# Masking on VectorE instead of TensorE: row maxima of batches 2 and 3 in layer 0 of a two-layer transformer kernel

## The reference

```python
qkv = jnp.einsum('bsd,od->bso', x, w_project)
...
att = jnp.einsum('bhqd,bhkd->bhqk', q, k) / math.sqrt(HEAD_DIM)
causal = jnp.triu(jnp.ones((s, s), dtype=bool), k=1)
att = jnp.where(causal[None, None, :, :], jnp.float32(-1000000000.0), att)
att = jax.nn.softmax(att, axis=-1)
out = jnp.einsum('bhqk,bhkd->bhqd', att, v)
```

## Time and profile before

| | |
|---|---|
| median of 3 runs | 256.35 us (256.03 to 258.0) |
| profiled execution, its own time | 255.42 us |
| its span (first to last instruction) | 253.5 us |
| TensorE matmuls busy | 240.6 us, 95% |
| TensorE weight loads busy | 216.3 us, 85% |
| VectorE busy | 204.3 us, 81% |
| ScalarE busy | 161.4 us, 64% |
| GpSimd busy | 167.1 us, 66% |
| mean granted clock of TensorE | 0.997 |

### The profile page before, as it was taken

One profiled execution on the slowest core, in us unless ns is written; L12 is line 12 of the kernel. 1 busy time (PEld: TensorE's weight loads), 2 busy tenths in 40 slices (PEclk: granted clock), 3 DMA queues, 4 the chain that ended last, 5 costly groups with the idle time before them and its releaser, 6 DMA issues.

```text
span 253.5 us, 6724 instructions
## 1 busy us (share of the span) xinstructions
PE 240.6 (95%) x2398; PEld 216.3 (85%) x2398; DVE 204.3 (81%) x599; ACT 161.4 (64%) x290; POOL 167.1 (66%) x218
## 2 busy tenths in 40 slices
PE   8998989999999999999999898998999999999991
PEld 8997967877789989989999897765788888999990
...
GB/s 164 277 193 203 216 175 241 152 120 79 76 98 109 109 129 119 85 145 144 187 85 189 3 122 189 31 153 145 0 45 3 4 3 0 3 35 8 3 0 124
DMA packets 23312, 26.39 MB, mean 104 GB/s; under 512 B 3184, under 2 KB 18288, under 8 KB 23280
## 3 DMA queue, kind: packets, MB, share of 16 engines
...
...
## 4 chain that ended last, share of the span: by engine, by line
PE 71%; POOL 6%; DVE 5%; DMA 5%; ACT 5%; issue 4%; SPq 2%; POOLq 0%; ACTq 0%
PE psum L566 9%; PE psum L567 8%; PE psum L568 8%; PE psum L686 6%; PE psum L661 5%; PE psum L741 5%; PE psum L742 5%; DMA k_stack<-k_part 3%; PE psum L629 3%; PE psum L689 2%; PE psum L633 2%; PE psum L664 2%; POOL hidden L1253 2%; PE psum L775 2%; PE psum L638 2%
## 5 line engine op out<-in xcount | busy, mean ns | idle before, releaser
L857 ACT ACTIVATE probs<-psum 128x768 f32<-128x768 f32 x64 | 49.1, 809 | 11.9 <-PE psum L667 5.9
L1253 POOL TENSOR_TENSOR hidden<-hf,hidden 128x512 fp32r<-128x512 f32 x24 | 31.6, 1320 | 13.5 <-ACT hidden L899 13.5
L1221 POOL TENSOR_SCALAR_AFFINE_SELECT probs<-probs 128x512 f32<-128x512 f32 x48 | 32.3, 688 | 10.1 <-ACT probs L857 9.7
L1009 DVE TENSOR_REDUCE block_max<-psum 128x6 f32<-128x768 f32 x32 | 28.9, 946 | 6.0 <-PE psum L633 5.9
L661 PE MATMUL psum<-q_stack,k_stack 98*128 98x256 bf16 x128 | 28.6, 274 | 2.1 <-DMA q_stack<-maxT_lo 1.0
L1020 DVE CUSTOM_DVE_ANT_0 masked<-psum,mask 128x256 bf16<-128x256 f32 x64 | 26.7, 418 | 1.6 <-issue 0.9
L1106 DVE SCALAR_TENSOR_TENSOR hf<-th,psum 128x512 f32<-128x512 f32 x28 | 18.9, 677 | 9.8 <-ACT th L888 3.9
L566 PE MATMUL psum<-xT_hi,gu_hi 128*128 128x256 f32 x88 | 25.3, 288 | 0.0
L567 PE MATMUL psum<-xT_lo,gu_hi 128*128 128x256 f32 x88 | 24.9, 283 | 0.0
L568 PE MATMUL psum<-xT_hi,gu_lo 128*128 128x256 f32 x88 | 24.9, 283 | 0.0
L664 PE MATMUL psum<-q_stack,k_stack 98*128 98x128 bf16 x128 | 24.7, 218 | 0.0
...
## 6 DMA issues: line engine op xcount, KB each, us to landing
q_stack<-q_part SPq DMA_DIRECT2D x48, 128.0 KB, 2.7
k_stack<-k_part SPq DMA_DIRECT2D x48, 128.0 KB, 2.4
...
```

Source lines behind the costliest of these rows:

```text
L857: nc.scalar.activation(probs[(n - 1) % 4][:, :, :], place(key)[:, :, 0:T + P], ACT.Exp, scale=SC).then_inc(exp_done, 1)
L1009: nc.vector.tensor_reduce(block_max[b % 2][:, 2 * i:2 * i + 2, 1:4], both(key)[:, :, 0:3 * P].rearrange("p j (c t) -> p j c t", t=P), mybi ...
L1221: pool.affine_select(out=diag, in_=diag, compare_op=ALU.is_ge, fill=0.0, base=0, pattern=[[0, 2], [0, 2], [1, P]], channel_multiplier=-1). ...
L1253: pool.tensor_tensor(hidden[(n - 1) % NHID][1][:, :, :], hf[n % 2][:, :].rearrange("p (a t) -> p a t", a=2), hidden[(n - 1) % NHID][0][:, ...
```

## The change

`MASKED_BY_PE` goes from 4 to 2. Batches 0 and 1 of layer 0 keep the mask by TensorE; batches 2 and 3 of layer 0 get the form that layer 1 has. On TensorE the third matmul of a head goes for 32 heads. On VectorE 16 reductions of two heads become 64 masked maxima, and MB:020 and MB:030 go. All five lists of steps and the table of banks are written anew, for layer 1 also. The steps in the lists are otherwise the same.

```diff
-MASKED_BY_PE = 4
+MASKED_BY_PE = 2
 TENSOR_STEPS = """
...
-    V:020 S:011-3 ST:000-1 S:014-5 ST:002-3 S:016 PV:000-1 ST:004-7 S:017 S:020-2 MX:010 PV:002-3 S:023-4 V:030
-    ST:010 S:025-6 ST:011 S:027 ST:012-4 MX:020 S:030 PV:010-1 S:031-2 ST:015 O:000 ST:016-7 ST:020 PV:012 S:033-4
-    ST:021 PV:013 ST:022 S:035-6 XT:000 ST:023 S:037 PV:020 ST:024-6 PV:021 MX:030 ST:027 GU:000 ST:030 PV:022-3
+    V:020 S:011-4 ST:000 S:015 ST:001-3 S:016 ST:004 PV:000-1 S:017 ST:005-6 S:020 ST:007 S:021 MX:010 S:022-3
+    PV:002-3 S:024-5 V:030 ST:010-2 S:026-7 ST:013 PV:010-1 ST:014 S:030 MX:020 S:031 ST:015-6 PV:012 S:032 ST:017
+    O:000 ST:020-1 PV:013 ST:022-4 S:033-6 PV:020 XT:000 S:037 PV:021 ST:025-7 MX:030 GU:000 PV:022-3 ST:030-1 O:010
...
 VECTOR_STEPS = """
-    XPARTS:000 PREPA:000-1 XPARTS:010 QK:000-1 XPARTS:020 XPARTS:030 QK:010 PREPA:002 QK:011 QK:020-1 PREPA:003
-    S:000-7 MB:000 S:010 MX:000 QK:030-1 S:011-6 SCALES:000 UT:000 IV:000 S:017 MB:010 S:020-1 MX:010 S:022 YM:000
-    S:023-4 UT:001 S:025-7 IV:001 MB:020 YM:001 YB:000 MX:020 S:030 UT:010 PREP0:004-5 S:031-2 O:000 PREP0:006
-    S:033-4 UT:011 S:035-7 MB:030 XT:000 MX:030 IV:010-1 YM:010-1 YB:010 GU:000 UT:020 IV:020 UT:021 YM:020 IV:021
+    XPARTS:000 PREPA:000-1 XPARTS:010 QK:000 PREPA:002-3 XPARTS:020 QK:001 QK:010-1 QK:020-1 XPARTS:030 S:000-7
+    MB:000 QK:030 S:010 MX:000 QK:031 S:011-5 SCALES:000 S:016 UT:000 S:017 MB:010 IV:000 S:020-1 MX:010 S:022-5
+    UT:001 IV:001 YM:000-1 S:026 YB:000 S:027 S:030 MX:020 UT:010 PREP0:004-5 S:031-2 O:000 PREP0:006 UT:011 S:033-6
+    IV:010 S:037 XT:000 YM:010 MX:030 IV:011 YM:011 YB:010 UT:020 GU:000 UT:021 IV:020-1 YM:020-1 YB:020 O:010
...
 SYNC_STEPS = """
-    LOAD:001 LOAD:003 QK:000 LOAD:002 QK:001 MID:000-1 LO:000-1 QK:010 MID:010 LO:010 MID:011 QK:011 LO:011 LO:020
-    RAW:000-1 LOAD:000 MX:000 ML:000 LO:021 QK:020 MID:020-1 QK:021 RAW:002-3 MID:030 QK:030 MX:010 ML:010 MID:031
-    LO:030-1 QK:031 RAW:004-5 ML:020 MX:020 RAW:006-9 MX:030 ML:030 RAW:0010-25 QK:100 RAW:0026-27 MID:100 QK:101
+    LOAD:001 LOAD:003 QK:000-1 LOAD:002 LO:000 MID:000-1 LO:001 LO:010 QK:010-1 MID:010-1 LO:011 RAW:000-1 LOAD:000
+    LO:020-1 MX:000 ML:000 QK:020 MID:020-1 QK:021 RAW:002-3 QK:030 MX:010 ML:010 QK:031 MID:030-1 LO:030-1
+    RAW:004-5 MX:020 ML:020 RAW:006-10 ML:030 MX:030 RAW:0011-25 LO:100 RAW:0026 MID:100 RAW:0027 QK:100-1 MID:101
...
```

More of the change, by code:

```diff
@@ new lines @@
+    MX:110 QK:131 ST:104 PV:100-1 ST:105 S:121 ST:106-7 S:122-4 V:130 S:125-6 PV:102-3 ST:110-1 S:127 ST:112-5
+    PV:110 MX:120 ST:116 PV:111 S:130-1 PV:112 S:132 ST:117 O:100 ST:120-1 S:133 PV:113 ST:122 S:134 ST:123 S:135
+    PV:120 ST:124 S:136 XT:200 ST:125-6 PV:121 S:137 GU:100 MX:130 ST:127 GU:101 PV:122-3 ST:130-1 O:110 ST:132-3
+    GU:102-3 ST:134 PV:130-1 D:100-1 ST:135-7 XT:210 D:102 O:120 GU:110 PV:132-3 GU:111-2 D:103 XT:220 GU:113 GU:120
+    D:110 O:130 GU:121 D:111-2 GU:122-3 XT:230 D:113 D:120 GU:130-1 D:121-2 GU:132-3 D:123 D:130-3
@@ L109 @@
 """
 SCALAR_STEPS = """
-    XPARTS:000 PREPA:000-1 QK:000 XPARTS:010 PREPA:002 QK:001 SPLIT:000 XPARTS:020 XPARTS:030 SPLIT:001 QK:010-1
-    SPLIT:010 QK:020 SPLIT:011 QK:021 PREPA:003 V:000 SPLIT:020-1 V:010 QK:030-1 MX:000 PREP0:000 V:020 SPLIT:030-1
-    PREP0:001 ST:000-7 MX:010 PREP0:002-3 V:030 ST:010-3 MX:020 YT:000 ST:014-5 PREP0:004-5 ST:016-7 ST:020
-    PREP0:006 ST:021 LN:000 ST:022 PREP1:000 ST:023 XT:000 ST:024-5 MX:030 ST:026-7 PREP1:001-2 GU:000 ST:030-2
-    YT:010 AB:100 HI:000 AB:101 ST:033 GU:001 YT:020 AB:102-3 GU:002 ST:034 LN:010 ST:035 HI:001-2 AB:104-5 ST:036-7
@@ L121 @@
-    ST:125-6 CV:105-7 MX:130 ST:127 GU:100 YT:110 GU:101 ST:130-1 HI:100-1 ST:132-3 GU:102 LN:210 GU:103 YT:120
-    XT:210 ST:134-7 HI:102-3 GU:110-1 LN:220 HI:110 GU:112 YT:130 GU:113 HI:111-2 XT:220 GU:120 HI:113 LN:300 LN:230
-    GU:121 HI:120-1 XT:230 GU:122-3 GU:130 HI:122 GU:131 HI:123 HI:130-1 GU:132-3 HI:132-3 LN:310 LN:320
+    XPARTS:000 PREPA:000-1 QK:000 XPARTS:010 PREPA:002 QK:001 SPLIT:000 PREPA:003 XPARTS:020 QK:010 SPLIT:001
+    SPLIT:010 QK:011 QK:020 SPLIT:011 XPARTS:030 QK:021 V:000 V:010 SPLIT:020 QK:030 SPLIT:021 MX:000 QK:031
@@ L124 @@
+    GU:120-1 HI:113 HI:120 LN:300 LN:230 XT:230 GU:122 HI:121 GU:123 HI:122 GU:130 HI:123 HI:130 GU:131-2 HI:131
+    GU:133 HI:132-3 LN:310 LN:320
 """
 VECTOR_STEPS = """
[L126 to L128 removed]
@@ new lines @@
+    YT:020 HI:001-2 ST:034-7 LN:020 LN:100 YT:030 HI:010 TERN:100 LN:030 TERN:101 HI:011-2 TERN:102 SPLIT:100
+    TERN:103 LN:110 TERN:104 HI:020 TERN:105 SPLIT:101 HI:021 TERN:106 SPLIT:110 HI:022 SPLIT:111 HI:030-1 LN:120
+    HI:032 PREP1:003 LN:130 SPLIT:120-1 TERN:107 XC:100 ST:100 XC:110 ST:101-6 TERN:108 ST:107 SPLIT:130-1 ST:110-5
+    YT:100 ST:116-7 ST:120-1 LN:200 ST:122-3 TERN:109 ST:124-6 XC:120 ST:127 YT:110 TERN:1010-11 HI:100 ST:130-3
+    HI:101 LN:210 HI:102 YT:120 ST:134-6 XC:130 ST:137 HI:103 LN:220 HI:110 YT:130 HI:111-2 LN:300 LN:230 HI:113
@@ L149 @@
+    HI:120-3 LN:310 HI:130-3 LN:320 LT:130-1
 """
 SYNC_STEPS = """
-    LOAD:001 LOAD:003 QK:000 LOAD:002 QK:001 MID:000-1 LO:000-1 QK:010 MID:010 LO:010 MID:011 QK:011 LO:011 LO:020
-    RAW:000-1 LOAD:000 MX:000 ML:000 LO:021 QK:020 MID:020-1 QK:021 RAW:002-3 MID:030 QK:030 MX:010 ML:010 MID:031
-    LO:030-1 QK:031 RAW:004-5 ML:020 MX:020 RAW:006-9 MX:030 ML:030 RAW:0010-25 QK:100 RAW:0026-27 MID:100 QK:101
-    MID:101 LO:100-1 RAW:0028-29 QK:110 RAW:0030 LO:110 QK:111 MID:110-1 LO:111 MX:100 ML:100 QK:120-1 MID:120-1
@@ L157 @@
+    LO:101 RAW:0028 QK:110 RAW:0029-30 LO:110 MID:110-1 QK:111 LO:111 MX:100 ML:100 QK:120-1 MID:120-1 LO:120-1
+    RAW:0031-32 ML:110 MX:110 QK:130 MID:130-1 QK:131 LO:130-1 MX:120 ML:120 RAW:0033-34 MX:130 ML:130 LN:300 LN:310
+    LN:320 LT:130-1
 """
 BANKS = """
[7 rows of a table removed]
[7 rows of a table added]
 """
```

57 lines of the change are left out of this document (24 added, 33 removed), and 14 rows, old and new, of the table BANKS.

## The result

The changed kernel took 258.1 us (median of 20 runs, 256.48 to 260.26), the kernel before 255.62 beside it (20 runs, 253.86 to 260.15). The ratio is 1.0103, interval 1.0078 to 1.0128: about 1% slower, where 256.1 us, no change, was forecast. (The ratio leaves out runs over 1.5% above the fastest of their kernel, such as the one of 260.15, and so isn't the quotient of the medians.) The time lies in the range. The profiled execution of the changed kernel has a span of 255.6 us and a time of 257.53; before, 253.5 and 255.42.

The account below looks back on a forecast made before the run. TensorE sets the pace if VectorE keeps up from 43 to 68 us. -3.5 (TensorE's work) + 3.3 (its wait at MX:030) + 0 (the rest) = -0.2, so 256.1 us from 256.35; range 252.9 to 258.7.

Parts of the forecast that it names:

- TensorE's work, -3.5: Batches 2 and 3 of layer 0: 32 mask matmuls fewer at 0.11 us per head, 3.5 us less on TensorE.
- VectorE's work, +3.5: Layer 0: 16 steps at 0.24 us more, 3.8, less 0.3 for two dropped joins; net +3.5 us.
- Batch 2, "it ends where it ended": Batch 2's 1.9 us more on VectorE, covered by an earlier start from 3.2 us of idle time; costed at nothing.
- S:030 on VectorE at 53.0 to 53.6: Start of batch 3's maxima in layer 0, against 53.23 us before; taken as 53.2.
- the +0.3: ST:007 on TensorE, behind S:017 and S:020 in the new order, comes 0.3 us later.
- rival 3: Slot hand-over: TensorE waits at S:020, ST:007 and batch 3's transfers slide; 258.3 or 260.2 us, chance 0.16 for over 258.9.
- The wait at MX:030, +3.3: TensorE reaches MX:030 near 64.8 us and waits over 3 us for VectorE's S:037; stretch ends at 68.1 for 67.94.
- Layer 1, 0 with +-3.85: All re-ordered parts: between 3.85 us of VectorE waits won and as much lost; taken as 0.
- Rival 2: By weight loads TensorE has room and its work sets nothing; 256.4 us, no change, chance 0.13.
- Rival 1: TensorE's saving arrives whole: 252.9 us, or 254.6 for half; chance 0.22 for under 253.8.
- Rival 4: The dealt orders of layer 1 alone move the time by over 2.5 us; chance 0.02 each way.

Follow-up runs that it names:

- orders_alone: The changed kernel with the mask of all of layer 0 by TensorE again, its new orders and banks kept; ratio 1.0100 to the kernel before.
- batch3_old_orders: The kernel before, orders and banks kept, with the mask of batch 3 of layer 0 alone taken by VectorE; ratio 1.0000.
- three filled kernels: The changed kernel with extra TensorE matmuls in waits: 18 or 9 ahead of S:030, or 9 there and 9 ahead of ST:000; ratios 1.0040-1.0044 to before.
- new_then_old: The changed kernel up to GU:000 on every engine, the orders and banks of the kernel before from there; ratio 1.0212.
- filled_both_before: The kernel before with 9 extra TensorE matmuls ahead of ST:000 and 9 ahead of S:030; ratio 1.0144.
- old_transfers: The changed kernel with SyncE's transfers for batch 3's stacks in the order of the kernel before; ratio 1.0033 to the kernel before.

## Why the prediction was wrong

Its sum was -3.5 + 3.3 + 0. The main step that failed is that the new orders cover batch 2's 1.9 us on VectorE for nothing: they were charged 0.3 us for a later ST:007 and 0 to 0.4 for later maxima, with S:030 on VectorE at 53.2. They do cover those 1.9 us, but orders_alone shows that they cost 1.0% by themselves. In the changed kernel's profile the first part of that is at S:030's start, where the landing of the last transfer was put at 2.4 us and took 4.0. L649 of MX:030 came at 70.52 for the 68.1 of the sum. Of these 2.4 us, 1.2 are S:030's start on VectorE, 0.5 the stretch from there to S:037's end, where the clock had no price, and 0.7 what lies between S:037's end and L649.

- **TensorE's work, -3.5.** The 32 matmuls went (L633 has 32 executions, L1020 and L1023 96 each). Busy time from 43 to 68 us is 21.96, near the 21.5 named. No run shows a gain from it: batch3_old_orders takes 1.6 us from TensorE and gains nothing.
- **VectorE's work, +3.5.** Right. The busy column shows only +1.8, but the maxima of layer 0 alone are busy for 32.7 us where they were for 28.9; other passes took less. The stretch from S:030 to the end of S:037 was put at 14.8 us and took 15.33 (54.37 to 69.70) with the clock low, and 14.7 in the three filled kernels.
- **Batch 2, "it ends where it ended".** In the changed kernel it did: VectorE was through with it at 51.95 and then idle for 2.40 us; the kernel before came to S:030 at 53.23. S:020 came 2.45 us earlier. What failed is "I cost it at nothing" for the cover. With the old orders VectorE is full at 10.20 of 10.23 us, and the form costs 1.0% in batch 2, part of it the clock; with the new orders that cost is hidden, and the orders cost 1.0%. They replace one loss by the other. I had feared batch 3, which costs nothing by itself, and read rows 2 over 25 us, where VectorE had 1.6 us to spare; over the 10 us ahead of S:030 it had 0.03.
- **S:030 on VectorE at 53.0 to 53.6.** It came at 54.37. ST:007's last L661 was 0.35 us later than before (40.69 for 40.34), as the +0.3 said, and the last issue was on time; the transfer took 4.0 us to land, and I had used the median of 2.4. It is the mechanism of rival 3, without its condition: TensorE didn't wait at S:020, and S:030 stayed under the 55.3 named there.
- **The wait at MX:030, +3.3.** The sum let TensorE run ahead to MX:030 by 64.8 us and stand there for 3.3. It didn't: it was held back on the way, by the clock and by short waits for banks (0.19 to 0.30 us, most of them for L1023), and its order has PV:021 and ST:025-7 behind S:037. It did these from 67.8 us on, the last after a wait for L1023 up to 69.93, and came to MX:030 at 70.52, 0.8 us after VectorE's end and not 0.1. In the filled kernels, with the clock up, the distance was 0.7 to 1.1.
- **The clock.** No step had a price for it. In the stretch behind S:030 it is the 0.6 us between 15.33 and 14.73. For the whole kernel the estimates differ: 0.7 us by the changed kernel's own runs, 1.5 us by the fillers.
- **Layer 1, 0 with +-3.85.** Right as a size for the changed kernel (-0.49 us behind MX:030), and by luck in part: new_then_old and filled_both_before show that 2 to 4 us can come and go there.

**The rivals.** Rival 2's claim, that TensorE's work sets nothing, isn't decided: batch3_old_orders (1.0000 with 1.6 us of it gone) fits it, but also fits the forecast's own mechanism, in which VectorE's added work takes up what TensorE saves. The time it gave, no change, was wrong. Rival 1 is out: no version with less work on TensorE came clearly under the kernel before. Rival 4 is out for the changed kernel.

What the runs show: the form in batch 2 and the new orders each cost the whole 1%, batch 3 costs nothing, and fillers that keep the clock up give 0.6% back. That all of these 0.6% are the clock isn't shown: the profiles and the changed kernel's own runs account for about half. The rest goes with the later S:030; no run takes that part away in the changed kernel. What stays open: why the last transfer lands late; why orders_alone loses 1.0% with no fall in its profile (mean clock 0.995, transfer in 2.4 us); whether old_transfers' 0.7% is due to the order of the transfers, since neither kernel built on it repeats it; and why filled_both_before is slow. A fourth slot for the stacks, which would take the hand-over away, wasn't tried. No version was found that beats the kernel before.
